# A graph network and expert kernel on one core: layer 1 with ten dense tiles in place of thirteen

## The reference

```python
def _gat(x, src, dst, W, a_src, a_dst, b, heads, ch, concat):
    h = (x @ W).reshape(n, heads, ch)
    es = (h * a_src).sum(-1)
    ed = (h * a_dst).sum(-1)
    e = jax.nn.leaky_relu(es[src] + ed[dst], SLOPE)
    m = jax.ops.segment_max(e, dst, num_segments=n)
    w = jnp.exp(e - m[dst])
    den = jax.ops.segment_sum(w, dst, num_segments=n)
    alpha = w / den[dst]
    msg = h[src] * alpha[:, :, None]
    out = jax.ops.segment_sum(msg, dst, num_segments=n)
    ...
x = x + gnn(layernorm(x), edges)          # two _gat layers, layernorm and relu between
x = x + ffn(layernorm(x))                 # top 2 of 8 experts
```

## Time and profile before

| | us |
|---|---|
| median of 3 runs | 1402.62 |
| lowest and highest run | 1395.42, 1405.33 |
| span of the profiled execution | 1413.3 |

### The profile page before, as it was taken

The page is one execution under the profiler, slowest core; times in us unless marked ns, Lnnn a source line. Parts: engine busy times, 40 slices in busy tenths (PEclk is TensorE's granted clock), DMA queues, the critical chain, the costliest instruction groups (busy, mean ns, idle before and its releaser), DMA issues.

```text
span 1413.3 us, 26112 instructions
## 1 busy us (share of the span) xinstructions
PE 1177.5 (83%) x8521; PEld 799.2 (57%) x8522; DVE 850.4 (60%) x2521; ACT 699.0 (49%) x1856; POOL 702.2 (50%) x621
## 2 busy tenths in 40 slices
PE   5677798889789988765878887783899999999997
PEld 3454232324233333344556555562799999999996
DVE  7799887889699878633666676677322222222222
ACT  4578576757567767632434333332334344334432
POOL 1003777667577751046666666610244445554543
PEclk9889998989899989967898999895899999999999
DMA  6136344634633651253464555523033342323222
GB/s 202 50 108 167 107 109 134 173 90 119 178 106 105 172 154 28 102 192 98 151 187 123 178 176 160 147 77 88 20 91 98 97 99 37 91 39 95 35 37 27
DMA packets 137157, 157.13 MB, mean 111 GB/s; under 512 B 58936, under 2 KB 116505, under 8 KB 137065
## 3 DMA queue, kind: packets, MB, share of 16 engines
q0 software_dynamic: 33616, 73.02, 21.9%
q1 hardware_dynamic: 102888, 82.42, 18.9%
q10 hardware_dynamic: 560, 0.52, 0.1%
HBM read 121.19 MB, written 35.52 MB: 111 GB/s over the span
## 4 chain that ended last, share of the span: by engine, by line
PE 44%; DVE 26%; issue 11%; ACT 5%; DMA 5%; another core or an unknown queue 5%; POOL 3%; DVEq 0%; POOLq 0%; ACTq 0%
PE bank L1499 11%; PE bank L1507 11%; PE bank L1368 8%; PE bank L1450 4%; DVE ring_a L1975 4%; DVE ohk L1720 3%; DMA out_x<-ring_a,si 3%; POOL arena L833 2%; ACT ring_a L1073 2%; DVE ohs L1716 2%; DVE ring_a L2035 2%; PE bank L1208 2%; PE bank L1310 2%; DVE st L1572 2%
## 5 line engine op out<-in xcount | busy, mean ns | idle before, releaser
L833 POOL DMA_INDIRECT arena<-rows,idx_e x365 | 398.5, 1092 | 308.3 <-issue 92.8
L1368 PE MATMUL bank<-ring_a,slots 128*64 128x384 f32 (+1 forms) x1600 | 276.4, 533 | 50.8 <-DVE ring_a L1975 33.3
L1450 PE MATMUL bank<-h2t,ring_a 128*128 128x257 f32 x700 | 191.7, 420 | 45.3 <-DVE ring_a L2035 23.8
L1073 ACT ACTIVATE ring_a<-vbb,slots 128x384 f32<-128x384 f32 x400 | 212.2, 605 | 11.9 <-DMA vbb<-v_rows 7.5
L1975 DVE SCALAR_TENSOR_TENSOR ring_a<-ring_a,arena 128x1536 f32<-128x1536 f32 (+1 forms) x125 | 192.4, 1540 | 28.8 <-ACT ring_a L1073 13.9
L1180 ACT ACTIVATE ring_a<-bank,cols 128x128 f32<-128x128 f32 x432 | 128.8, 371 | 160.4 <-PE bank L1499 160.1
L1450 PEld LDWEIGHTS bank<-h2t,ring_a 128*128 128x128 f32 x700 | 139.3, 209 | 80.1 <-issue 34.4
L1368 PEld LDWEIGHTS bank<-ring_a,slots 128*64 128x64 f32 (+1 forms) x1600 | 60.9, 125 | 118.2 <-DVE ring_a L1975 52.8
L879 POOL DMA_INDIRECT gs<-gates,gk x54 | 51.3, 949 | 152.2 <-DVE gk L2127 138.4
L1499 PEld LDWEIGHTS bank<-ring_a,arena 128*128 128x128 f32 x1056 | 123.1, 192 | 1.7
L1499 PE MATMUL bank<-ring_a,arena 128*128 128x128 f32 x1056 | 123.2, 275 | 0.0
(11 more groups left out here) (313 smaller groups left out, 1756.1 us busy)
## 6 DMA issues: line engine op xcount, KB each, us to landing
counts_all<-arena SPq DMA_DIRECT2D x14, 800.0 KB
arena<-counts_all SPq DMA_DIRECT2D x14, 800.0 KB
arena<-in_L_ffn_W SPq DMA_DIRECT2D x8, 1024.0 KB, 7.6
vbb<-v_pairs SPq DMA_DIRECT2D x23, 320.0 KB
arena<-rows,idx_e POOLq DMA_INDIRECT x365
XB<-general_sums SPq DMA_DIRECT2D x38, 130.0 KB
vbb<-in_L_ffn_W SPq DMA_DIRECT2D x4, 1024.0 KB
spare<-in_L_ffn_W SPq DMA_DIRECT2D x4, 1024.0 KB
```

Source lines behind the costliest of these rows:

```text
L833: pool.indirect_dma_start(to[:, k, 0:width], None, table, bass.IndirectOffsetOnAxis(idx_e[:, m * PAIR + k:m * PAIR + k + 1], 0)).then_inc( ...
L1073: ins = act.activation(S1[q % SLOTS1][:, h * k * P:(h + 1) * k * P].rearrange("p (t n) -> p t n", n=P), (vb1 if b else vb0)[:, 0:k, h, :], ...
L1368: ins = pe.matmul(to, weights, S1[q % SLOTS1][:, h * w_:(h + 1) * w_], start=(s == 0), stop=(s == NT - 1))
L1450: ins = pe.matmul(bank[(j % 2) * 2 + i][:, 0:W2T], S2[q2 % SLOTS2][:, i * P:(i + 1) * P], h2t[:, s, 0:W2T], start=(s == 0), stop=(s == NT ...
```

## The change

`NE` goes from 13 to 10. Layer 1 has four dense blocks (100 steps); tiles 10 to 12 join the edge tiles, which makes 15 edge tiles and 58 pairs, 290 gathers. The pairs start at step 26 and are spread over 72 steps. Tile 13 is counted with tiles 1 to 3 in block 0 (four visits a step there, in place of three) into the space behind tile 0's counts, and stored ahead of SP's step loop; tiles 10 to 12 are still counted, in the steps of the last block, and stored at step 101. Block 0 scales two tiles of the table a step. The loads of general sums stand at norm - 2 in place of norm - 6. Normalised edge tiles rotate over four rows of `orow` in place of two, and the router's small arrays move into `XE`. The steps run on to 126 (`END1`); tiles 22 to 24 take their turns at 108, 110 and 112, tiles 7 to 9 at 114, 116 and 118, and norm stands at 104, 106 and 108 for tiles 7 to 9.

```diff
-NE, ND = 13, 14
+NE, ND = 10, 14
 CB = ((0, 1),) + tuple((t, min(3, ND - t)) for t in range(1, ND, 3))
 B1 = CB[:1 + NE // 3]
+SIDE = (0, 1, 0, 1, 0, 0)
+STORED = (0, 5, 1, 2, 3, 4)
...
+COUNTED = ((0,), (1, 2, ND - 1, 3)) + tuple(tuple(range(t, t + 3)) for t in range(4, ND - 1, 3))
+AT = {t: n for n, t in enumerate(t for tiles in COUNTED for t in tiles)}
...
-        VISITS_AT.setdefault((_b - 1) * NT + _n // PER_STEP, []).append((_w, _v, _u))
+        VISITS_AT.setdefault((_b - 1) * NT + _n // (PER_STEP + (_b == 1)), []).append((_w, _v, _u))
...
-PAIR1 = [28 + p * 86 // PAIRS for p in range(PAIRS)]
+PAIR1 = [26 + p * 72 // PAIRS for p in range(PAIRS)]
...
 def edge_row(t):
-    return 3 + (t - NE) % 2
+    return 3 + (t - NE) % 4
...
-        orow = sb("orow", [P, 5, D])
+        orow = sb("orow", [P, 7, D])
...
+        at1 = [SIDE[b] * 9600 + (NT * P if b == len(B1) + 1 else 0) for b in range(len(CB))]
...
             store_counts(0)
+            store_counts(len(CB) - 1)
             for q in range(END1):
                 if q % NT == 0 and 1 < q // NT < len(B1):
                     block_rows(q // NT)
-                if q % NT == 1 and 0 < q // NT < len(CB):
+                if q % NT == 1 and 0 < q // NT < len(CB) - 1:
                     store_counts(q // NT)
-                for g, i, t in tiles_at(G1, norm_of, q, -6):
+                for g, i, t in tiles_at(G1, norm_of, q, -2):
                     if g.dense:
...
-                        if work:
+                        while len(work) >= PASSES - i:
                             visit(*work.pop(0))
...
-                    if b == 0 and s + 2 < NT:
-                        scale(s + 2)
+                    for t in range(2 * s + 2, min(2 * s + 4, NT)) if b == 0 else ():
+                        scale(t)
```

66 lines of the change are left out of this document (32 added, 34 removed).

## The result

| | before | after |
|---|---|---|
| median of the runs, us | 1400.55 | 1450.39 |
| lowest and highest run, us | 1395.42, 1405.33 | 1441.26, 1451.41 |
| span of the profiled execution, us | 1413.3 | 1449.7 |
| layer 2's first gather starts at, us | 614.40 | 652.57 |

The kernel became slower: ratio 1.0344, 95% interval 1.0301 to 1.0388. I had forecast 1412.6 us, with a range up to 1440. From layer 2's first gather to the end of the span nothing changed (1413.3 - 614.4 = 798.9 us before, 1449.7 - 652.6 = 797.1 after), so the loss lies where the prediction looked for it. The two traces differ by 38 us there, the medians by 50.

A forecast was written before the change was run, and what follows sets the result against it. GpSimd's gathers were taken to bound layer 1's long stage. Earlier start -5.7, gathers +25.6, last gather to last matmul -29.4 and end +19.8 made 10 us later, added to the 1402.62 median: about 1412.6 us, range 1388 to 1440.

The forecast's parts named there:

- part 1: Block 0: first gather moves from 125.30 to 110.6 us, sixteenth starts at 143.4; 5.7 us of the earlier start are left.
- part 2: Layer 1's pairs: 275 gathers against 215, at 1.51 us each, set the pace; last gather ends at 558.7 us.
- With room: Layer 1's pairs: VectorE (about 327 us of work), TensorE and ScalarE follow the gathers without setting the pace.
- The slower rival: Layer 1's pairs: 1.60 us a gather, layer 2 starting at 649, 35 us later, 1437 us; chance 0.36.
- the ring of three buffers: Layer 1's pairs: a gather waits for the visit of the pair three earlier; GpSimd waits as today, 13%.
- part 3: End of layer 1: loads of general sums queue behind count and weight loads on SP; 43 us in place of 23.2.
- from last gather to last matmul: End of layer 1: landing, a pair's weights, steps 96 to 99 and TensorE's last pass take 23 us, for 52.4 before.
- the forecast's lower bound: End of layer 1, last dense matmul to layer 2's first gather: 29 us if tile 8's load is not held.
- The share of the turns: End of layer 1: turns of tiles 22 to 24 on VectorE add 6 us, some 3 of their 9 being hidden.
- the upper end of the range: Layer 1's gathers at 1.61 us each: layer 2 starts at 652, 38 us later, median 1440.
- The Trainium skill's rule: Layer 1's gathers: only two-port VectorE copies and tensor-scalar operations stop them; 68 us of holds stay, end at 567, 8 later.

The follow-up runs named there:

- the short multiplication: Changed kernel, VectorE's multiplication by the counts cut to 2 of each 128 destinations after block 0; only traced: gather stretch 435.0 us against 440.8.
- a fourth buffer: Changed kernel with four instead of three buffers of gathered rows in layer 1; 1439.00 us, ratio 1.0322 to the kernel before.

## Why the prediction was wrong

*The start (part 1): right.* First gather 111.4, forecast 110.6; sixteenth 145.3, forecast 143.4. The gain is 3.8 us, forecast 5.7.

*The pairs (part 2): the step that failed.* It read "So the gathers set the pace, and VectorE, TensorE and ScalarE follow with room", and took 1.48 us a gather with its holds and 2% for waits, 1.51. Measured is 1.502 with holds and 0.10 of waits, 1.603. That the gathers set the pace came near, with GpSimd's own time at 94% of the stretch; that the others follow with room failed. Of the 25.5 us, 6 are holds and 20 are waits (27.8 in place of some 8). The holds were 67 us in place of 61, because they did not shrink with the number of steps: 67 gathers began inside the multiplications of 69 steps, and 68 inside those of 79 steps before.

The mechanism of the holds was right: with the short multiplication they went from 67 to 10 us. What I did not see is that holds and waits take each other's place. Earlier normalisations turned 17 us of waits into 14 of holds, the short multiplication 58 us of holds into 52 of waits, and a fourth buffer lowered neither. In the runs with 275 gathers their sum is 88 to 109 us, less only where nine of a pair's products were left out (73), while each by itself ranges from 10 to 88 (holds) and 11 to 80 (waits). As the sum is the stretch less a fixed amount, this says that something beside GpSimd holds the stretch near 440 us. So it was wrong to give the holds a price and let the waits vanish.

"With room" was wrong for TensorE, and could have been seen. Its issue gaps belong to its time just as GpSimd's 0.30 does, which I did count. Busy time and gaps fill 88% of the stretch in after, where holds were removed 94 to 95%, and in the trace that the prediction was made from they already filled 89%. For VectorE the sum of its work was right (324.6 us, forecast 327), but its order has no room: 75.6 us of waits at the pairs' weights, none before. How the 20 us divide between TensorE, its lower clock (0.93 before, 0.88 after) and VectorE's order with its two buffers of pairs' weights is not settled: cutting TensorE's columns lowered the clock, so that its part can't be had alone, and the buffers were not varied.

*The slower rival* had 1.60 us a gather and layer 2's start at 649 (measured 652.6), but by the ring of three buffers; a fourth buffer left the waits as they were, and they were 6% of the stretch and not the 13% of before. That its number fits is luck. It was said to decide from 1.53 a gather on, 14 us above now; by the prediction's own terms that point is 16 us above.

*The end (part 3): right in size, and for the most part in cause.* From last gather to last matmul 23.5 us, forecast 23; the end 42.9, forecast 43. With the loads ahead of the counts it was 28.0, where the forecast's lower bound had 29. That 43 came out to the tenth is luck: the second tile's sums came 21 us after the matmuls, forecast 18, and the rest took 22, forecast 25. The share of the turns was not tried.

*The sum.* In the traces: start -3.8, gathers +51.1, from last gather to last matmul -28.9, end +19.7, together +38.1; forecast -5.7, +25.6, -29.4, +19.8. The median moved by 50. The remaining 12 us are the base: I added a difference of traces to the median, as if the profiled execution of after would stand as far above its median as that of before. It did not (0.7 us below, against 12.8 above). In the traces the upper end of the range, 1.61 a gather and layer 2's start at 652, was met almost exactly; by the base alone the median came out beyond 1440.

*The Trainium skill's rule* gave an end of the gathers at 567 by holds that stay at 68 us whole. They did stay (67.4), but not for its reason: the cut of the two-SBUF multiplication removed them, the cut of the one-hots did not, and the gathers that begin inside a one-hot take 0.97 us.

## What to carry to other kernels

Count an engine's own gaps into its time, for every engine of a stage, before saying that one sets the pace and the others follow with room; where two are near 90%, don't let today's waits go to nothing: the 1.60 measured here lies between the forecast's 1.51, with hardly any, and today's 1.81, with all of them. Look also at which buffers tie two engines together once the work comes closer: here the two buffers of pairs' weights, which cost no wait before. When a wait is taken away, look at whether the engine's next instructions got longer, not only whether the wait is gone. And a load of data that is needed soon must not stand behind a bulk prefetch on the same queue: moving three such loads ahead took 15 us out of the end of layer 1.

## What the runs showed of the hardware

- What holds an indirect gather on GpSimd here is a multiplication of two SBUF operands on VectorE: gathers that begin inside it take 1.86 us in the mean, those that begin inside a 16-bit one-hot 0.97, those that begin with VectorE idle 0.95.
- The granted clock moved with TensorE's work: with three quarters of the columns of two passes out it was 0.77 and 0.79 in place of 0.88, and in the first of these a record of the untouched pass took 655 ns in place of 554; with 58.5 us of work added it was 0.93.
- Products into 64 of 128 columns ran beside each other: one head of two took 0.86 us, both 0.87. So did the four heads of a pair's visit: one took 0.43 us, all four 0.44.
- The last products of a pair, 24 records in a row, mostly take 0.52 us in after. In the run with the short multiplication 29 of 58 such groups took over 1.5 us, against 8 of 58 in after, and all small products of the stretch took 99.5 us and 45.2 of issue gaps, against 83.2 and 18.6. There they come apart with gaps that the profile puts to issue:

```profile
484.03 0.66 PE L1322 MATMUL bank<-arena,ring_a 128*32 128x65 f32 x10
485.12 0.27 PE L1322 MATMUL bank<-arena,ring_a 128*32 128x65 f32 x2 [0.42 <-issue]
```

What holds them there was not found. In that run the DMA engines were as busy during the long groups (0.61) as during the short ones (0.59), but the longest group of after, 9 us from 452 us on, falls where they were at 1.12, so their load is not ruled out.
